# A decoder layer on one core: the copy of a group's sums set right behind the exp, and the work in front of slot 0 regrouped

## The reference

```python
k, v, q = x @ Wk.T + bk, x @ Wv.T + bv, x @ Wq.T + bq          # 128 wide
# scan over t: out_t = state @ q_t ; state = 0.99 * state + 0.01 * outer(v_t, k_t)
x = layernorm(x + outs @ Wo.T + bo)
# cross attention with ctx_1024, 16 heads of 16, then output projection
x = layernorm(x + softmax(qh @ kh.T / 4) @ vh  @ w_o.T + b_o)
# self attention, 16 heads of 16, plus a mixture of 8 experts, 2 chosen per row
attn = softmax(q3 @ k3.T / 4) @ v3
gate = softmax(x @ W_gate + b_gate); combine = top-2 of gate
x = layernorm(x + attn + sum_e combine_e * (x @ W_experts[e] + b_experts[e]))
```

## Time and profile before

| what | value |
|---|---|
| time, median of 3 runs | 1263.95 us (1262.15 to 1264.09) |
| the profiled execution | 1261.23 us, its span 1259.4 us |
| mean granted clock of PE | 0.996 of full speed |
| busy: PE, DVE, ACT, POOL | 96%, 73%, 62%, 30% of the span |
| first score (slot 0) | at 70.17 us |

### The profile page before, as it was taken

The page is one execution under the profiler, slowest core; times in us unless marked ns, Lnnn a source line. Parts: engine busy times, 40 slices in busy tenths (PEclk is TensorE's granted clock), DMA queues, the critical chain, the costliest instruction groups (busy, mean ns, idle before and its releaser), DMA issues.

```text
span 1259.4 us, 20675 instructions
## 1 busy us (share of the span) xinstructions
PE 1207.8 (96%) x7004; PEld 601.2 (48%) x7004; DVE 918.7 (73%) x1867; ACT 778.6 (62%) x1090; POOL 381.9 (30%) x485
## 2 busy tenths in 40 slices
PE   8789999999999999999999999999999999999998
PEld 4443444545445445444454454454454544544443
DVE  3587786678777787777877777777777778678772
ACT  2255556665576665766657665667557666665664
POOL 5510103411622134420523206231153204430261
PEclk9899999999999999999999999999999999999999
DMA  7422122112222122222122222122122211212200
GB/s 249 117 56 65 43 52 66 46 46 56 62 67 58 39 68 56 56 69 51 46 66 66 57 58 65 44 72 52 39 56 69 52 36 43 68 28 52 52 18 18
DMA packets 56446, 74.99 MB, mean 60 GB/s; under 512 B 14720, under 2 KB 26520, under 8 KB 56088
## 3 DMA queue, kind: packets, MB, share of 16 engines
q1 hardware_dynamic: 55192, 72.96, 23.2%
q10 hardware_dynamic: 1152, 0.72, 0.2%
HBM read 18.06 MB, written 4.19 MB: 18 GB/s over the span
## 4 chain that ended last, share of the span: by engine, by line
PE 80%; DVE 7%; ACT 6%; issue 4%; SPq 2%; DMA 1%; POOL 0%; ACTq 0%; DVEq 0%
PE ms L480 36%; PE op L480 16%; PE sc L480 15%; PE mx L480 9%; DVE maxes L984 3%; PE ms L590 2%; ACT probs L798 2%; SPq L427 2%; PE ms L531 2%; ACT moe L791 1%; PE ms L585 1%; DVE q_parts L894 1%; ACT k_parts L734 1%; ACT q_parts L734 0%; ACT oT L733 0%
## 5 line engine op out<-in xcount | busy, mean ns | idle before, releaser
L984 DVE TENSOR_REDUCE maxes<-mx 128x1 f32<-128x512 f32 x1024 | 657.7, 684 | 209.4 <-PE mx L480 207.6
L798 ACT ACTIVATE probs<-sc 128x1024 f32<-128x1024 f32 x512 | 525.1, 1026 | 365.2 <-PE sc L480 361.2
L1234 POOL TENSOR_TENSOR x<-x,moe 128x256 f32<-128x256 f32 x256 | 187.5, 732 | 653.8 <-ACT moe L791 632.2
L480 PE MATMUL op<-probs,v 128*32 128x512 f32 x2048 | 272.8, 604 | 7.1 <-ACT oT L733 6.8
L480 PE MATMUL sc<-qs,ks 50*128 50x512 f32 x1024 | 256.3, 497 | 12.0 <-ACT probs L798 11.1
L480 PEld LDWEIGHTS sc<-qs,ks 50*128 50x128 f32 x1024 | 95.3, 183 | 304.7 <-ACT probs L798 232.4
L480 PE MATMUL mx<-ks,qs 48*128 48x512 f32 x1024 | 209.7, 404 | 13.5 <-DVE maxes L984 12.5
L791 ACT ACTIVATE moe<-ms,comb 128x256 f32<-128x256 f32 x256 | 107.0, 473 | 24.0 <-PE ms L480 24.0
L480 PEld LDWEIGHTS mx<-ks,qs 48*128 48x128 f32 x1024 | 97.4, 187 | 25.5 <-DVE maxes L984 20.5
L480 PE MATMUL ms<-we_hi,x2T_hi 128*128 128x512 f32 x256 | 92.8, 443 | 3.2 <-DVE q_parts L894 1.0
L480 PEld LDWEIGHTS op<-probs,v 128*32 128x32 f32 x2048 | 40.7, 108 | 100.9 <-issue 99.3
(11 more groups left out here) (155 smaller groups left out, 1303.9 us busy)
## 6 DMA issues: line engine op xcount, KB each, us to landing
ks<-k_parts SPq DMA_DIRECT2D x384, 64.0 KB, 2.3
qs<-q_parts SPq DMA_DIRECT2D x381, 64.0 KB, 2.2
xT_s<-in_xT SPq DMA_DIRECT2D x8, 512.0 KB, 3.9
x_s<-in_x SPq DMA_DIRECT2D x8, 512.0 KB, 4.3
out<-x SPq DMA_DIRECT2D x7, 512.0 KB, 3.2
x_s<-in_ctxT SPq DMA_DIRECT2D x6, 512.0 KB, 5.1
qs<-shift_r SPq DMA_DIRECT2D x128, 8.0 KB
x<-in_ctxT SPq DMA_DIRECT2D x2, 512.0 KB, 6.4
```

Of the source, the lines that this page charges most:

```text
L480: return nc.tensor.matmul(dst, lhsT, rhs, start=first, stop=last, skip_group_check=True)
L798: nc.scalar.activation(probs[:, (2 * s + h) % 3, :, :], sc[:], ACT.Exp).then_inc(exp_out, 1)
L984: nc.vector.tensor_reduce(maxes[:, g % 2, at:at + 1], mx[:, i % 3, :], AX_X, ALU.max).then_inc(max_out, 1)
L1234: nc.gpsimd.tensor_tensor(x2[:, n % 2, t, :], x2[:, n % 2, t, :], moe[:, k % 2, j * D:j * D + D], ALU.add).then_inc(acc, 1)
```

## The change

Four things move. On ACT, a group's copy `oT<-op` stands right behind the exp of its half, in front of the take-outs (of groups that are not `wanted`). On PE, units in front of slot 0 are emitted in their own half, right behind the two pairs or one pair of maxima of that half, and a filler stands only in halves that have no unit. On DVE, units of `EARLY_OUT` in front of slot 0 are taken out in front of the maxima in both halves. In the tables `qc1` of batch 0 and `k1`, `s0`, `s1`, `s23`, `o1`, `y01`, `y23` of batch 1 come a half to a slot or more earlier, and batch 1's `ctx_high` comes eight slots later, from (-12, 1) to (-4, 1).

```diff
-             "x1": (-16, 0), "qc0": (-15, 0), "cv1": (-15, 1), "kc1": (-14, 1), "qc1": (-6, 1),
+             "x1": (-16, 0), "qc0": (-15, 0), "cv1": (-15, 1), "kc1": (-14, 1), "qc1": (-6, 0),
-LIN_SECOND = {"q1": (-13, 1), "k1": (-5, 1), "v1": (-14, 0), "s0": (-4, 1), "s1": (-3, 0), "s23": (-3, 1),
+LIN_SECOND = {"q1": (-13, 1), "k1": (-6, 1), "v1": (-14, 0), "s0": (-5, 1), "s1": (-4, 0), "s23": (-4, 1),
...
-              "ctx_high": (-12, 1), "ctx_low": (-3, 0)}
+              "ctx_high": (-4, 1), "ctx_low": (-3, 0)}
@@ PE
-                if -MAX_LEAD <= s < 0 and not (h == 1 and UNITS[t - 1] + UNITS[t]):
+                if -MAX_LEAD <= s < 0 and not UNITS[t]:
                     busy(1, T // 2)
@@ PE
-                if h == 0:
+                if s < 0:
+                    for task, n in UNITS[t]:
+                        unit(task, n)
+                elif h == 0:
@@ ACT
                     exps(s, h)
+                for task, k, n in OTHERS["act"][t]:
+                    if task == "oT" and not wanted(k):
+                        other(task, k, n)
                 for task, n in units:
                     if not first_out(task, n):
                         high(task, n) if task in SPLITS else take_out(task, n)
                 for task, k, n in OTHERS["act"][t]:
-                    if not (task == "oT" and wanted(k)):
+                    if task != "oT":
                         other(task, k, n)
@@ DVE
-                first = [unit for unit in units if h == 0 and unit[0] in EARLY_OUT or first_out(*unit) or
+                first = [unit for unit in units if (h == 0 or t < 0) and unit[0] in EARLY_OUT or first_out(*unit) or
```

## The result

The changed kernel takes 1252.52 us (median of 4 runs, 1249.89 to 1253.78); the kernel before takes 1263.05 us in the same comparison (4 runs, 1262.07 to 1264.09). The ratio is 0.991, with a 95% interval of 0.9892 to 0.9929: 11.4 us faster, with bounds of 9.0 and 13.6. The profiled execution took 1252.54 us with a span of 1250.8 us, 8.6 us shorter than the span before. Forecast were 1252.0 us and a gain of 11.8 us.

What follows compares the result with a forecast made beforehand. PE's own work bounds the kernel (busy 96%), leaving 51.6 us of idle time to win. Front 6.4 plus copy 5.4 gives 11.8 us: 1263.95 - 11.8 = 1252.1, say 1252 us, range 1248 to 1259.

Steps and rivals of the forecast that it cites:

- the front term: In front of slot 0, up to slot 1's last maxima: 6.4 us won, with bounds of 3.5 and 7.6.
- the copy: Batches, ACT's `oT` copy: seven places win 0.66 us each, three small waits 0.8 us together, 5.4 us in all.
- Step 1: PE, front: first pair of maxima stays at 39.77 us; `qc1` follows, 3.58 us at half clock, ending at 43.8.
- Step 2: ACT and DVE, front: `q1` copied from 44.1 us; DVE's low part of `q_parts` ends at 46.2 instead of 52.2.
- Step 3: PE, front: `k1` takes 1.98 us, ending at 46.8; third pair of maxima near 47.1 us instead of 52.84.
- the clock stays low: Rival, 14%: PE's clock stays at half in front of slot 0; one long stretch costs 3 us, 1255 us; all, 1259.5.
- Step 4: DVE, front: from 47.3 us, 22.9 us of work and 1.5 idle; slot 1's last maxima end at 71.7, not 78.1.
- Steps 5 and 6: PE, front: first score at 63 us; group 0's shift arriving late costs nothing, at worst 0.9 us beside DVE's backlog.
- Step 7: ACT and POOL, front: batch 1's context copies, now behind `k1` on ACT, cost nothing, with 7 us of cover.
- three signs of being wrong: Clock near 0.55 over 4 us behind 46 us; DVE idle over 4 us before slot 2; new PE waits on take-outs.
- PE at clock 1.00 from 46 us on: Expected profile sign: PE's granted clock is full from 46 us on.
- no wait over 1.5 us on maxima: Expected profile sign, front: PE waits at most 1.5 us on DVE's maxima before the first score, near 63 us.

Runs made afterwards that it cites:

- pool_later: The changed kernel with POOL's low parts of batch 1's context waiting for DVE's first shift: ratio 0.9916 to the kernel before, 1252.48 us.
- ctx_early: The changed kernel with batch 1's `ctx_high` put back from (-4, 1) to (-12, 1): ratio 0.9951 to the kernel before, 1259.01 us.
- front_only: The changed kernel with the group's copy on ACT put back behind the take-outs: ratio 0.9954 to the kernel before, 1257.72 us.
- fillers: The changed kernel with two more filler matmuls of 512 columns in each half of slot -6: ratio 0.9894 to the kernel before, 1249.93 us.
- w3_fill: w3_later with the extra filler matmuls of fillers in slot -6: ratio 0.9888 to the kernel before, 1250.04 us.
- w3_later: The changed kernel with ACT's last two weight copies moved behind batch 0's `q_parts`: ratio 0.9872 to the kernel before, 1246.87 us.
- copy_only: The kernel before with only the new place of the group's copy on ACT: ratio 0.9945, 1256.38 us.
- w3_alone: The kernel before with only its last two weight copies on ACT moved to `k1`'s slot: ratio 0.9998, 1264.26 us.
- w3_again: The same kernel as w3_later, measured again on another chip: ratio 0.9893 to the kernel before, 1248.28 us.
- w3_ctx: The kernel before with the group's copy, context copies and last two weight copies moved, units and fillers as before: ratio 0.99, 1251.68 us.
- both: w3_later with the POOL wait of pool_later added: ratio 0.9883 to the kernel before, 1248.74 us.
- ctx_only: The kernel before with only batch 1's `ctx_high` moved from (-12, 1) to (-4, 1): ratio 0.9954, 1258.58 us.

## Why the prediction was right, point by point

The total and both of its terms came out in the medians. In the profiled execution the front term did not: the steps that failed there are 3 and 4, with `k1` behind a wait on ACT and at half clock, and with DVE held by POOL.

*The sum.* 11.8 us were forecast and 11.4 (9.0 to 13.6) measured, with both terms inside their intervals: the copy 5.4 against 6.9 (5.2 to 8.7) by ratio and 5.4 to 5.9 by the traces' rest, the front 6.4 against 5.8 (4.4 to 7.2). Against the profiled execution I was further off: a span of 1247.6 us was forecast and 1250.8 measured, a time of 1249.4 and 1252.54. Of what was said to stay, ACT's and POOL's busy times did; DVE's grew by 4.1 us.

*The copy.* Right in mechanism and size: the 0.83 us at each place became 0.17 us on the exp. The later take-outs cost nothing; no wait of `ms` on `moe` or `lin` take-outs has grown into the large lines.

*Step 1* (`qc1` on PE) came out 1.1 us early: the first pair stood at 40.32 us and not at 39.77 (it stands between 39.47 and 40.48 us in the traces without extra fillers), but `qc1` ran at full clock and ended at 42.7 where I had 43.8.

*Step 2* (ACT and DVE through `q_parts`). Right to 0.3 us: `q1` was copied at 44.39 us (44.1 forecast), DVE's low part ended at 46.43 (46.2).

*Step 3* (`k1` ends at 46.8 us) failed by 1.4 us in the profiled execution. `k1` started at 45.12 us, 0.3 us late, and took 3.06 us where I used the 1.98 us of a stretch at full clock. I had this as a rival, "the clock stays low", with a price of 3 us for one such stretch, and gave it 14%. It is no alternative to the forecast: it happens in some executions and not in others. Four traces have the change's units with ACT late; there `k1` took 3.06 (the change), 3.62 (pool_later), 2.67 (ctx_early) and 1.98 us (front_only) behind waits of 1.89 to 2.43 us. In the ten others that wait was 0.82 us or less (in fillers and w3_fill with filler matmuls in its place), and it took 1.98 or 1.99 us each time. What I should have seen: I kept `qc1` at its half clock, 3.58 us, and so it seemed to end just before ACT was ready. At full clock PE is through with `qc1` and the second pair at 43.17 us and waits 1.95 us for ACT's weight copies, which could have been moved.

The Trainium skill, "TensorE: Matmul & The Clock Gate", section "What's actually happening", has it that the throttled clock is the default and activity releases it. The traces agree in direction, by the count just given, though `qc1` below shows that the waits alone do not decide it. The rows decide how much that is worth, the rule does not.

*Step 4* (slot 1's last maxima at 71.7 us) failed by 3.6 us: they ended at 75.3. DVE started 2.34 us later than the 47.3 us forecast (step 3's 1.4 us, and the filler and the pair behind `k1` at the low clock). The window from there to the end shows the other 1.3 us:

```profile
49.64:75.32 25.68, 20.15 (x83) 9.80 (x87) 24.25 (x45) 6.36 (x8) 12.34 (x11) 0.93 0.36 87
```

Idle time is 1.43 us, as I put it (1.5), and the busy time 24.25 in place of 22.9. The two held shift instructions make 1.9 us of it (2.24 in place of 0.34), and without them my list would have been 0.55 us too long. In w3_later these maxima ended at 69.6 us and the first score came at 61.88, before my 71.7 and 63.

*Steps 5 and 6.* The first score was forecast at 63 us and came at 67.69: 1.4 us of that is step 3, and behind it stand the two stretches of low clock and PE's wait of 1.00 us for the held shift; how much of the rest each of them makes, no run separates. That the arrival of the shift costs the first score nothing was right: DVE wrote `shift_n` by 60.97 us, and the first score at 67.69 us waited for nothing.

*Step 7* said that POOL's context parts cost nothing, since POOL stands at 58.04 us with 7 us of cover. As to when they are needed this is right. But I moved DVE's list 5 us earlier over a POOL list that stands still, and asked only who waits for POOL, not what runs beside it. The shift pair moved from 60.71 us, just behind POOL's end, to 58.70, into its last two instructions. In the traces the pair took 0.34 us where POOL was idle (before, copy_only, ctx_early, pool_later, w3_alone), 0.85 to 1.69 us where it met `w_lo` or `x_s` (w3_later, w3_again, w3_ctx, both, w3_fill, front_only, ctx_only), 2.24 us on `ctxT_lo` (the change) and 4.14 us over both in fillers. The Trainium skill, "SBUF — State Buffer", section "Who interferes with whom", describes such a hold: VectorE and GpSimd share a port pair as an exclusive lock, taken by copies and tensor_scalar in their two-port modes and, against a GpSimd instruction that reads, by instructions with two SBUF inputs. A TENSOR_SCALAR and an instruction with two inputs are here, and the trace agrees for both: their ends lie 0.03 to 0.05 us behind POOL's. In which mode the TENSOR_SCALAR ran, no row shows. The maxima, which read PSUM, kept their 1.26 to 1.29 us for two beside POOL. By that section of the Trainium skill the one that waits goes on when the other's instruction has ended; in fillers it waited over several, and the measurement decides. I could have read all this from the trace before, at 379.61 us. What it costs in the median, pool_later could not show.

*The regrouped units.* I took steps 1 to 4 as one thing and gave it 6.4 us. Of its two parts the context copies' move brings all that the runs can show, and the units none of it; with ACT freed of the weight copies they likely bring something.

*The signs.* *"PE at clock 1.00 from 46 us on"* and *"no wait over 1.5 us on maxima"*: the first was wrong in this execution (0.70 in two of the windows above), the second right (1.17). The wait on the exp grew by 1.7 us where I had said about 1, and the busy time of DVE was said to stay the same. Of the three signs of being wrong, two showed in this trace. PE has a new wait on an `x1T` take-out, the 1.95 us in front of `k1`. And the clock was at 0.55 over 3.1 us from 46.5 us on and at 0.52 over 3.5 us from 63 us on, which is more than 4 us if the two are taken together:

```profile
46.50:49.60 3.10, 3.10 (x6) 1.06 (x5) 0.00 (x0) 0.69 (x1) 3.02 (x2) 0.55 0.75 197
63.00:66.50 3.50, 3.50 (x9) 2.13 (x8) 2.71 (x5) 0.00 (x0) 0.00 (x0) 0.52 0.23 55
```

The third, over 4 us of idle time on DVE, did not (1.43). So the number came out with the mechanism of the front only partly as forecast.

*Why the median fits better than the trace.* The profiled front gained 2.8 us, but the median gain of front_only and ctx_only is 5.8 us. The fronts of one list differ between executions: PE's list of the kernel before stood at 79.09, 80.86 and 83.00 us at the sixth score (before, copy_only, w3_alone, the last with two copies on ACT moved), the change's at 73.34 and 76.26 (front_only, the change). I took the front's gain against one execution and 2.7 us for the difference to the median; that came out, but with a spread of 3 to 4 us in each front it was also luck, all the more as steps 3 and 4 failed in the trace against which I had added them up.

## What to carry to other kernels

In an engine's list, look for what needs a load in front of what another engine waits for; one number that moved two copies behind `q_parts` was worth half of the whole change. When a list is moved earlier over an engine whose work is tied to loads, ask what it now runs beside, on shared ports too, and which wait of the new order stands directly ahead of long matmuls. A regrouping that wins nothing may lack one more move: look at the largest new single wait in front of it, as here at PE's 1.95 us on ACT, and take that away before judging.

## What was not expected of the hardware

- A small VectorE instruction can be held over several GpSimd instructions in a row: 3.96 us for 128x16 elements that otherwise take 0.17 us, up to the end of the last of them. Holds of up to 1.21 us also stand at eight places of the kernel before.
- The same list of PE with waits of the same order got its full clock in one execution and not in another: `qc1` in the order before took 3.58, 3.48 and 3.25 us in three traces (before, w3_ctx, w3_alone) and 1.98 us in two (copy_only, ctx_only), behind waits of 1.0 to 1.6 and 0.75 us each time. What decides it, no run here shows.
- Far from any change, the window from 1170 to 1190 us had a granted clock of 1.00 in seven traces, 0.91 in four and 0.83 in three, and the rest of the span goes by it. With the copy's new place it is 1174.4 to 1175.9 us at 1.00, 1176.5 and 1177.0 at 0.91 (w3_ctx, w3_fill), 1177.5 and 1179.1 at 0.83 (fillers, both). Without it, it is 1180.3 at 1.00 (before), 1181.2 and 1181.3 at 0.91 (w3_alone, front_only) and 1183.6 at 0.83 (ctx_only). So the copy's gain is 4 to 6 us at equal clock. That part of the spread of runs is made there too is likely; runs without a trace cannot show it.
